# Eight expert blocks from an early count, run behind the last gate

## What is computed

```python
x = x + _L0_ffn_ref(_L0_cond_ref(x, cond_128, ...), W_gate, b_gate, W_e, b_e)
x = x + _L1_ffn_ref(_L1_cond_ref(x, cond_128, ...), qweight, scales, zeros, bias)
# L0_cond: grouped 9-tap convolution, plus a context per sample and channel
# L0_ffn:  logits = h @ W_gate + b_gate; the best 2 of 8 experts of each token;
#          relu(h @ W_e[e] + b_e[e]) for those two, averaged
# L1_cond: a small network gives 8 weights per sample, which mix 8 kernels of 32x32
#          (and 8 biases) into one per sample; it is applied over the channels
# L1_ffn:  int4 weights, W = scales * q - zeros; out = h @ W + bias
```

## Time and profile before

| | |
|---|---|
| median of the runs shown | 547.59 us |
| the profiled execution, its own time | 549.46 us |
| its span, first to last instruction | 547.7 us |
| busy TensorE, VectorE, ScalarE, GpSimd | 519.4, 339.4, 121.8, 144.0 us |
| expert products (L989) | 230.8 us |
| mean granted TensorE clock | 0.978 |

### The profile page before, as it was taken

One profiled execution on the slowest core, in us unless ns is written; L12 is line 12 of the kernel. 1 busy time (PEld: TensorE's weight loads), 2 busy tenths in 40 slices (PEclk: granted clock), 3 DMA queues, 4 the chain that ended last, 5 costly groups with the idle time before them and its releaser, 6 DMA issues. The chain is left out here.

```text
span 547.7 us, 10445 instructions
## 1 busy us (share of the span) xinstructions
PE 519.4 (95%) x2486; PEld 349.3 (64%) x2487; DVE 339.4 (62%) x1003; ACT 121.8 (22%) x277; POOL 144.0 (26%) x162
## 2 busy tenths in 40 slices
PE   6969999999979999999999999999968999999996
PEld 5969999999956444444444444444436667777774
DVE  3466888888873653333333333334753699999996
ACT  2122223324410111111111111111131222222221
POOL 8042444444462000000000000000006655555520
PEclk9999999999978999999999999999988899999999
DMA  4999778887344844444444444444476788888852
GB/s 114 378 312 343 249 251 277 291 281 258 139 166 155 214 159 154 153 153 153 153 153 153 153 153 153 153 153 154 138 247 180 222 277 288 279 278 287 294 183 96
DMA packets 84823, 114.32 MB, mean 209 GB/s; under 512 B 15197, under 2 KB 51853, under 8 KB 83509
## 3 DMA queue, kind: packets, MB, share of 16 engines
q1 hardware_dynamic: 57936, 56.49, 33.0%
q0 software_dynamic: 10528, 33.75, 18.1%
q10 hardware_dynamic: 16328, 23.72, 12.3%
HBM read 67.48 MB, written 46.45 MB: 208 GB/s over the span
## 5 line engine op out<-in xcount | busy, mean ns | idle before, releaser
L989 PE MATMUL bank<-we,hT 128*128 x536 | 230.8, 593 | 1.2 <-DVE hT L815 1.2
L989 PEld LDWEIGHTS bank<-we,hT 128*128 128x128 f32 x536 | 101.5, 190 | 129.4 <-issue 129.2
L454 POOL DMA_INDIRECT we<-result_d,gidx x64 | 65.4, 1021 | 292.0 <-issue 288.5
L824 DVE TENSOR_TENSOR ring_a<-bank,be_bc 128x512 f32<-128x512 f32 x71 | 48.9, 690 | 125.5 <-PE bank L989 116.2
L957 PE MATMUL bank<-wconv,phases 128*128 128x128 f32 x768 | 94.2, 281 | 4.8 <-issue 4.1
L957 PEld LDWEIGHTS bank<-wconv,phases 128*128 128x128 f32 x768 | 91.4, 197 | 5.3 <-issue 4.3
L532 ACT ACTIVATE ring_b<-ring_a 128x512 f32<-128x512 f32 x71 | 44.9, 632 | 206.7 <-DVE ring_a L824 200.0
L435 POOL DMA_INDIRECT lists_d<-htok,row_i x64 | 62.9, 982 | 87.8 <-issue 63.4
L815 DVE STREAM_TRANSPOSE hT<-htok 128x512 f32<-128x512 f32 x71 | 49.9, 702 | 8.3 <-DMA htok<-lists_d 8.3
L1029 PE MATMUL bank<-mix_bd,we 128*128 128x128 f32 x256 | 36.7, 288 | 4.6 <-DVE we L868 3.4
L1029 PEld LDWEIGHTS bank<-mix_bd,we 128*128 128x128 f32 x256 | 32.0, 196 | 11.2 <-DVE we L868 10.0
(11 more groups left out here) (164 smaller groups left out, 410.8 us busy)
## 6 DMA issues: line engine op xcount, KB each, us to landing
htok<-lists_d SPq DMA_DIRECT2D x284, 64.0 KB, 2.4
result_d<-ring_b ACTq DMA_DIRECT2D x71, 256.0 KB, 2.5
xt<-in_x SPq DMA_DIRECT2D x64, 256.0 KB
we<-in_L_ffn_W_e SPq DMA_DIRECT2D x8, 1024.0 KB
out<-orow SPq DMA_DIRECT2D x32, 256.0 KB
lists_d<-orow SPq DMA_DIRECT2D x8, 256.0 KB
be_bc<-in_L_ffn_b_e ACTq DMA_DIRECT2D x1, 2048.0 KB
rows_r<-ctx_d SPq DMA_DIRECT2D x1, 1920.0 KB, 10.9
```

Source lines behind the costliest of these rows:

```text
L454: pool.indirect_dma_start(found[:, j, k, :], None, result_d, bass.IndirectOffsetOnAxis(ap=gidx[:, j, k:k + 1], axis=0), bounds_check=NT * ...
L824: dve.tensor_tensor(ring_a[:, j % 2, :], ps_exp[j % 2][:, :], be_bc[:, bass.ds(expert, 1), :].rearrange("p a n -> p (a n)"), ALU.add).then ...
L989: mm = pe.matmul(ps_exp[j % 2][:, :], hT[:, j % 2, p * P:(p + 1) * P], we[:, bass.ds(expert, 1), p, :].rearrange("m a n -> m (a n)"), star ...
```

## The change

Slots 0 to 7 are filled from counts taken before the end. After 15 groups are counted, VectorE works out how many full blocks of 128 rows each expert has by then, and takes the first eight of them, in 18 small operations spread over its groups 16 to 26 (`early_table`). SyncE loads these blocks as soon as the slots of `xt` are free (`xt` takes the place of `htok` as the buffer of the lists), and VectorE transposes them between the last groups (`transpose_list`), into `lT`, which has four slots and shares two with `hT`. TensorE runs product 0 right behind the last gate; the last two counts of ranks, the mix matmuls and the table's transpose stand between products. The final table leaves out the blocks taken. The 34 transposes are gone. Transposes of lists run two slots ahead instead of one.

Since an expert's rows now lie in two pieces, `find_places` goes over two edges for each expert, 16 in all, and it is compared with the row instead of with the expert. The side work moves later: nothing in slots 1 to 3, the last half of the nibbles at slot 60, the column sums behind product 60, `find_places` at slots 65 to 67. The loads of x for stage 3 wait until the last list is transposed. Groups 16 to 23 of stage 1 are written out instead of looped. `mlp_first` keeps the small network at group 24.

```diff
+EARLY = 8
+AHEAD = 4
...
-        hT = sb("hT", [P, 2, L])
+        lT = sb("lT", [P, AHEAD, L])
+        hT = lT[:, 2:4, :]
...
-        lo1, hi1 = U, NG - 2 * U
+        lo1, hi1 = U, NG // 2
+        mlp_first = NG - 2 * U
+        snap = hi1
+        counted = snap - 1
+        N_EARLY = 18
...
-                a = s + 3
+                a = s + U
                 if live(a, NT):
-                    ja = (j + 3) % U
-
-                    sp.reg_load(row_reg, tab[0:1, bass.ds(a, 1)])
+                    ja = j
+                    if isinstance(a, int) and a == EARLY:
+                        sp.wait_ge(head_out, 16 * E)
+                        for i, scat in enumerate(scattered):
+                            sp.wait_ge(scat, 32 * len(range(i, NG, U)))
+                        sp.wait_ge(tab_ready, 2)
+
+                    if isinstance(a, int) and a < EARLY:
+                        sp.reg_load(row_reg, tab_early[0:1, 0, a:a + 1])
+                    else:
+                        sp.reg_load(row_reg, tab[0:1, bass.ds(a - EARLY, 1)])
                     row = sp.snap(row_reg, min_val=0, max_val=E * REGION - P)
-                    wait(sp, lT_ready, a - 3)
+                    if isinstance(a, int) and a < XR:
+                        sp.wait_ge(xT_ready, NG - XR + a + 1)
+                    else:
+                        wait(sp, lT_ready, a - XR + 1)
 
                     for mh in range(MH):
-                        sp.dma_start(htok[mh * B:(mh + 1) * B, ja, :].rearrange("r (h n) -> r h n", h=MH),
+                        sp.dma_start(xt[mh * B:(mh + 1) * B, ja, :].rearrange("r (h n) -> r h n", h=MH),
                                      lists_d[bass.ds(row, P), mh * P:(mh + 1) * P].rearrange("(h r) n -> r h n", r=B)
                                      ).then_inc(list_in[ja], 16)
 
-            stepped(sp, list_step, -3, lo2, hi2 - U, NT - 3)
+            stepped(sp, list_step, -U, lo2, hi2 - U, NT - U)
+            sp.wait_ge(lT_ready, NT)
...
+            for s in range(lo2):
+                step2(s, s % U)
+                if s == 4:
+                    store_mix()
+                if s == 6:
+                    load_mix()
+            stepped(act, step2, lo2, lo2, hi2, NT)
...
+            def early_table(step):
...
+                if step == 0:
+                    dve.wait_ge(base_ready, counted)
+                    early_op(dve.tensor_tensor(tint[:, :], base[:, :], region[:, :], ALU.subtract))
...
+                if step == 10:
+                    early_wait()
+                    early_op(dve.scalar_tensor_tensor(tab_early[:, 0, :], slot_e[:, :, 0:1].rearrange("p t a -> p (t a)"), float(P), early_sum[:, 0, :], ALU.mult, ALU.add),
+                             dve.tensor_scalar(tab_early[:, 1, :], early_sum[:, 1, :], -1.0, None, ALU.add))
...
+            def step1_late(g, j):
+
+                step1(g, j)
+                if snap <= g <= snap + 10:
+                    early_table(g - snap)
+
+            def transpose_list(a, ja):
+
+                wait(dve, list_in[ja], (a - ja) * (64 // XR) + 64)
+                wait(dve, exp_done, a - AHEAD + 1)
+                dve.transpose(lT[:, ja, :].rearrange("m (p h r) -> m h p r", p=PH, h=MH),
+                              xt[:, ja, :].rearrange("r (h p l) -> r h p l", h=MH, p=PH)).then_inc(lT_ready, 1)
+
+            def add_bias(s, j):
+
+                if isinstance(s, int) and s < EARLY:
+                    expert = dve.value_load(tab_early[0:1, 1, s:s + 1], min_val=0, max_val=E - 1)
+                else:
+                    expert = dve.value_load(tab[1:2, bass.ds(s - EARLY, 1)], min_val=0, max_val=E - 1)
+                wait(dve, exp_done, s + 1)
+                wait(dve, result_ready, s - 1)
+                dve.tensor_tensor(ring_a[:, j % 2, :], ps_exp[j % 2][:, :],
+                                  be_bc[:, bass.ds(expert, 1), :].rearrange("p a n -> p (a n)"), ALU.add).then_inc(sum_ready, 1)
+
+            stepped(dve, step1, 0, lo1, hi1, hi1)
+            for g in range(hi1, NG - 2):
+                step1_late(g, g % U)
+            assert n_early[0] == N_EARLY
+            early_wait()
+            transpose_list(0, 0)
+            step1(NG - 2, (NG - 2) % U)
+            transpose_list(1, 1)
+            step1(NG - 1, (NG - 1) % U)
+            dve.wait_ge(tok_done, NG - 1)
+            transpose_list(2, 2)
+            step1(NG, NG % U)
+            dve.wait_ge(tok_done, NG)
+            transpose_list(3, 3)
+            dve.wait_ge(be_in, 16)
+            add_bias(0, 0)
+            step1(NG + 1, (NG + 1) % U)
+            add_bias(1, 1)
...
+            transpose_list(4, 0)
+            add_bias(2, 2)
...
+            transpose_list(5, 1)
+            add_bias(3, 3)
...
+            def place_steps():
+
+                then(dve.scalar_tensor_tensor(late_from[:, :], early_taken[:, :], float(P), region[:, :], ALU.mult, ALU.add),
+                     dve.tensor_scalar(late_offs[:, :], offs[:, :], float(-P * EARLY), None, ALU.add))
+                then(dve.tensor_tensor(to_late[:, :], late_offs[:, :], early_offs[:, :], ALU.subtract),
+                     dve.tensor_copy(to_early[:, 0:1], early_offs[:, 0:1]),
+                     dve.tensor_tensor(to_early[:, 1:E], early_offs[:, 1:E], late_offs[:, 0:E - 1], ALU.subtract))
...
-                    if e == 0:
-                        then(dve.tensor_scalar(shift_s[:, :], expert2, 0.0, offs[:, 0:1], ALU.is_equal, ALU.mult))
-                    else:
-                        then(dve.tensor_scalar(shift_e[:, :], expert2, float(e), offs[:, e:e + 1], ALU.is_equal, ALU.mult))
-                        then(dve.tensor_tensor(shift_s[:, :], shift_s[:, :], shift_e[:, :], ALU.add))
+                    for edge, change in ((region, to_early), (late_from, to_late)):
+                        if e == 0 and edge is region:
+                            then(dve.tensor_scalar(shift_s[:, :], rows2, edge[:, e:e + 1], change[:, e:e + 1], ALU.is_ge, ALU.mult))
+                        else:
+                            then(dve.tensor_scalar(shift_e[:, :], rows2, edge[:, e:e + 1], change[:, e:e + 1], ALU.is_ge, ALU.mult))
+                            then(dve.tensor_tensor(shift_s[:, :], shift_s[:, :], shift_e[:, :], ALU.add))
...
+                if live(s + AHEAD - 2, NT):
+                    transpose_list(s + AHEAD - 2, (j + AHEAD - 2) % U)
...
-            side_work = {1: rank_masks, 2: odd_even, 3: nibble_shifts, 4: lambda: nibbles(0), 5: lambda: nibbles(2),
-                         7: rank_sums, hi2: rank_rows, hi2 + 1: rank_split, hi2 + 2: lambda: find_places(0, 3),
-                         hi2 + 3: lambda: find_places(3, 6), hi2 + 4: lambda: find_places(6, E)}
-
-            stepped(dve, step2, -1, lo2, hi2, NT)
+                    add_bias(s, j)
+
+            side_work = {4: rank_masks, 5: odd_even, 6: nibble_shifts, 7: lambda: nibbles(0), hi2: lambda: nibbles(2),
+                         hi2 + 1: rank_sums, hi2 + 2: rank_rows, hi2 + 3: rank_split,
+                         hi2 + 4: place_steps, hi2 + 5: lambda: find_places(0, 3),
+                         hi2 + 6: lambda: find_places(3, 6), hi2 + 7: lambda: find_places(6, E)}
+
+            stepped(dve, step2, 4, lo2, hi2, NT)
...
-            pe.wait_ge(tab_ready, 1)
-            pe.transpose(ps_misc[0:3, 256:256 + P], tab_f[:, :], ident[:, :]).then_inc(tab_done, 1)
-
-            for _ in range(WARM):
-                pe.transpose(bank[6][:, 0:P], ident[:, :], ident[:, :])
-            pe.wait_ge(tab_ready, 2)
-            pe.wait_ge(we_in, 16 * E)
...
-                if isinstance(s, int) and s == 6:
+                if isinstance(s, int) and s == hi2:
...
-            stepped(pe, step2, 0, lo2, hi2, NT)
+            gate_and_rows(NG - 1, (NG - 1) % U)
+            pe.wait_ge(early, N_EARLY)
+            pe.wait_ge(we_in, 16 * E)
+            product(0, 0)
+            count_ranks(NG - 2, (NG - 2) % U)
+            product(1, 1)
+            count_ranks(NG - 1, (NG - 1) % U)
+            mix_layers(NG + 1 - mlp_first)
+            for s in range(2, 5):
+                product(s, s % U)
+            pe.wait_ge(tab_ready, 1)
+            pe.transpose(ps_misc[0:3, 256:256 + P], tab_f[:, :], ident[:, :]).then_inc(tab_done, 1)
+            for s in range(5, EARLY):
+                product(s, s % U)
+            pe.wait_ge(tab_ready, 2)
+            stepped(pe, step2, lo2, lo2, hi2, NT)
```

More of the change, by code:

```diff
@@ L147, in build_program @@
         tab = sb("tab", [3, P], I32)
+        slot_e = sb("slot_e", [1, EARLY, E])
+        early_start = sb("early_start", [P, E])
+        early_taken = sb("early_taken", [P, E])
+        early_offs = sb("early_offs", [P, E])
+        early_step = sb("early_step", [P, E])
+        early_mask = sb("early_mask", [1, EARLY, E])
+        early_prod = sb("early_prod", [1, EARLY, E])
+        early_sum = sb("early_sum", [1, 2, EARLY])
+        tab_early = sb("tab_early", [1, 2, EARLY], I32)
```

(12 more changed lines are left out.)

129 lines of the change are left out of this document (78 added, 51 removed).

## The result

The changed kernel takes **551.61 us** (median of 20 runs, 549.28 to 553.89), the kernel before 548.35 us beside it (20 runs, 545.86 to 551.18). The ratio is **1.0055**, 95% interval 1.004 to 1.0071: about 3 us slower. The forecast was 548.2 on a kernel before of 547.59, a loss of 0.6 us. The sign is right, the size is not. The first turn gave what was forecast within half a microsecond; the second cost 1.5 us more. The profile shows one of the quicker executions of the changed kernel (549.62 us by its own time, the second lowest of 20, at a mean granted clock of 0.975, which no other exceeds; over all 20 the clock averages 0.971), so the typical one has some 2 us on top that no profile shows.

What follows compares the result with a forecast made beforehand. TensorE was taken to bound the middle of stages 1 and 2, with the turns apart. Gain 8.6, less clock 1.5 and second turn 7.8, gave -0.7: 548.2 us on a median of 547.59, range 543.0 to 552.5 (8 in 10).

Steps and rivals of the forecast that it cites:

- Product 0 early: First turn: product 0 follows the last gate, removing 14.27 us; loading the first expert's number still costs 0.5 us.
- the rival that it doesn't start early: First turn: late inputs keep product 0 near 170, so the tail is lost without a gain; 555.4 us, chance 0.04.
- Stage 1 free: Stage 1: VectorE's 18 added operations fit in its idle time and cost nothing; about 3 us if not covered.
- First turn: From last gate to product 7: 14.27 us removed, 5.7 us remaining, a gain of 8.6 us (7.3 to 11.5).
- The stall: Ahead of product 6: TensorE waits 2.85 us for VectorE's late bias step of slot 4 (0 to 4.1).
- The clock: Behind the stall ahead of product 6: half clock for about 3.4 us, costing 1.5 us (0 to 5.1).
- The second turn, VectorE: Slots 61 to 67: VectorE at 0.263 us per operation puts bias step 67 at 33.8 us; 7.0 us lost.
- Transfers, the mis-sized term: Second turn, bias step 67 to first gather: x loads beside the last writes add 0.8 us (nothing to 2.3).

Runs made afterwards that it cites:

- late lists in `htok`: The changed kernel with the lists of slots 8 to 70 loaded into `htok` again and SyncE's wait ahead of the x loads removed; 548.70 us, ratio 1.0005.
- stall filled: The changed kernel with 26 transposes that nobody reads on TensorE ahead of product 6; 551.29 us, ratio 1.0042 against the kernel before.
- the three together: The changed kernel with rank masks in slot 5, late lists in `htok`, and side work eight slots sooner with places under products; 536.83 us, ratio 0.9787.
- places spread: The changed kernel with late side work eight slots sooner and `find_places` in four pieces, a slot free between pieces; 544.23 us, ratio 0.9906.
- masks later: The changed kernel with the rank masks moved from slot 4 to slot 5 and two small constant steps together in slot 6; 549.43 us, ratio 1.0025.
- additional warm matmuls: The three together with 52 instead of 42 unread matmuls ahead of stage 3 and 8 more behind its first mix; 538.39 us.
- before with its places late: The kernel before with only `find_places` moved from slots 62 to 64 to slots 65 to 67; 550.43 us, ratio 1.0024.

## Why the prediction was right, and where it was short

- **Product 0 early**: 0.32 us behind the last gate, forecast 0.5. Right; the rival that it doesn't start early is out.
- **Stage 1 free**: the pitch is 4.18, as forecast, and the 103.2 us from group 8 to the last gate are those of the kernel before.
- **First turn**: what stands between gate and product 6 besides six products is 5.85 us (182.37 - 155.94 - 6 x 3.43), forecast 5.7. The stall is 2.72 (2.85 forecast), for the reason given. The step of slot 59 comes 7.9 us sooner, counted from the last gate (221.8 before, 213.85 after). The forecast was 8.4 (14.27 - 5.7 - 1.5, and 1.3 for the column sums, which moved behind step 59).
- **The clock**: 3.4 us at half clock behind the stall, costing 1.61; forecast 1.5. The size is right for the changed kernel's profile, and that is partly luck: the same stall left the clock up in two of the three profiles that hold it unfilled.
- **The second turn, VectorE**: step 67 at 34.15 behind step 59, forecast 33.8. The steps of slots 65 and 66 took 5.41 and 5.67 instead of 4.96 and 5.23: each operation takes 0.30 ((5.41 - 2.07) / 11), not 0.263. `shift_e` takes 0.31 where it took 0.25, as the two rows below show, the first from VectorE's timeline before, the second from the one after. It now reads both of its scalars from memory (edge and change), where before one was a constant, and it compares in another way; no run parts the two. I priced the new operation by the old one's time. Two errors the other way hid it: the steps of slots 61 to 64 came 0.5 us sooner than forecast (18.63 behind step 59 instead of 19.1), and step 67's 4.44 is the forecast number by luck, since with nine operations of 0.30 it would be 4.8, but its last wait was 0.59 and not 0.85.

```profile
391.97 0.25 DVE L798 TENSOR_SCALAR shift_e<-expert_of,offs 128x64 f32<-128x64 f32 x1
391.19 0.31 DVE L948 TENSOR_SCALAR shift_e<-row_of,late_from,to_late 128x64 f32<-128x64 f32 x1
```

- **Transfers, the mis-sized term.** From step 67 to the first gather it is 10.32 us (414.26 - 403.94) instead of 8.32. I took +0.8, and it is **+2.0**, close to the upper end of +2.3 that the two writes of before gave. The last write is issued 3.4 us behind the first load of x (408.73 - 405.28) and pays 4.49; the write at 404.08 before stood 3.3 us behind it (404.08 - 400.75) and paid 4.36. The row for it was there; I shaded it down without a reason. The late lists in `htok` confirm it: the write back at 2.05, and 2.4 us back. The mechanism is rather a shared transfer rate than a slower single access: from 407 to 412 the DMA engines are busy at a share of 0.8 to 1.2 and move 291 to 410 GB/s, and with the late lists, where the same four writes run alone, 0.4 to 0.7 and at most 256 GB/s. The Trainium skill, "DMA: Bandwidth & Descriptors", section "Latency and other measured facts", gives DRAM access at high load as 2 us against 0.2 on average. The estimate from it, up to 1.8, is nearer to +2.0 than my value, but the write itself grew by 2.5 us here and by up to 3.7 (5.73 with the stall filled), so the access time alone doesn't account for it.

The three shortfalls, 0.4 at the first turn, 0.35 and 1.2 at the second, make 2.0 of the 2.1 us between the forecast -0.7 and the yardstick's -2.8. A forecast of -0.7 was the difference of two large terms, 8.6 won and 9.3 lost, so a right sign is worth little here; what carries the prediction is that each term was found in its place. One slip of arithmetic: by its own terms the first gather stands 42.9 us behind product 59 (33.8 + 8.3 + 0.8), not 42.7; it is 44.5. The second turn took back 9.4 us (10.72, from 44.47 against 33.75 behind step 59, less 1.3 for the column sums). Of these, 7.1 come back when the same work is spread, and 2.4 when the loads of x are early.

What stays open is when the clock falls. Each fall of the first turn costs about 1.65 us (1.61 and 1.69). The profiles show it at two places without a clear condition, and none in the three together, the late lists and the filled stall. Open too is what the typical execution of the changed kernel, with a mean granted clock lower by 0.004, has beyond the one profiled.

## What to carry to other kernels

An early start is worth what it removes only if the work that stood in the gap finds cover elsewhere: list the side work of each other engine against the products left, and move the late part first. Here the start alone cost half a per cent, the same start with the side work spread won about 1%, and with all three edits about 2%. When a buffer gets a second use, look at which later transfers wait for it, and price a transfer that will meet the last writes by a write of the trace that already meets one.

## What the runs showed of the hardware

- **Half clock isn't decided by one idle time alone.** Behind an idle time of 2.72 to 2.73 us in dense products the granted clock fell to 0.50 in the changed kernel, but not with the late lists in `htok` nor with the places spread. With the masks later, the places spread, and the additional warm matmuls it fell with no idle time just ahead, for some 3.4 us, in products 2 to 4 (with the masks later at about 169.3, where the last idle time, 0.35 us, had ended at 159.78), right behind the mix matmuls, which have only 8 rows of input. The other four profiles of the changed order hold the same matmuls without a fall, so whether they are the cause is not shown.
- **A 256 KB write beside the first loads of x takes over twice as long.** The last write takes 2.02 to 2.06 us where the first of those loads is issued 8.4 us or more ahead of it (before, before with its places late, late lists, the three together, more warm matmuls), and 4.49 to 5.73 where it is issued 3.4 to 3.7 us ahead (after, masks later, stall filled, places spread). The late lists, which differ from the changed kernel in the buffer and in that wait alone, show it as the cause.
